# Moving the fetch of the rows' terms and of the first three row tiles from behind the second group's distances to between their stores

## The chip, the cores and the metric

One core of one Trainium2 chip runs the whole program. The metric is device time of one execution in microseconds (us), the median of several runs.

## What is computed

A latent array `x` (32 sequences of 64 rows of 256 numbers) is aligned with a context (32 sequences of 1601 rows of 256), and then passes a recurrence and a mixture of experts. The change lies in the first part, the alignment:

```python
D = sqrt(max(|a|^2 + |b|^2 - 2 a b^T, 0))           # 64 x 1601 distances for each of the 32 sequences
R[i, j] = D[i, j] + min(R[i-1, j], R[i, j-1], R[i-1, j-1])
# the way back: from (63, 1600) to (0, 0), each time to the smallest of the three neighbours
expanded[j] += a[i]   for every (i, j) on the way
x = x + expanded                                     # a = the context rows, summed per latent row
x = x + recurrence(layernorm(x))
x = x + experts(layernorm(x))                        # 8 experts, top 2, and a shared one
```

With the shapes of this case each latent row receives the sum of the context rows that the path matches with it: the "path sums".

## The kernel before, in words

The 32 sequences are worked in two groups of 16, and each group in 32 **units** (u = 0 to 31 for the first group, 32 to 63 for the second). A unit is a pair of sequences and a quarter of the 1601 columns. Per unit:

- SyncE (SP) loads transposed context columns into one of a few `ctxT` tiles; one load (two DMAs, one per sequence) serves two units. In the second group two slots alternate, so a load can only be issued when ScalarE's squares and TensorE's products of the two units that used the slot before are done (`load_next`, which runs at the odd units of SP's loop).
- ScalarE (ACT) squares the columns (`sq`, L1444), TensorE (PE) forms the products (L1734, and L1740 with the squares), and ACT takes the roots (`distance_roots`). PE then subtracts (L1780, L1781) and VectorE (DVE) corrects (L845, `z`) and adds (L861, `dist`).
- SP stores the distances to DRAM (`spaced`, L2226), and loads them back in the layout of the alignment (`table`, L2241).

DVE works through the alignment of the group: 71 steps forward (`align`: L948 the minimum, L959 the scan, L908 `stays`, L914 `code`), then 71 steps of the way back (L977, L978, L984), then `path_features`, which ends in `path_terms` (L1053). Its order is written out by hand: the second group's distances alternate with the first group's `align(0)`, one piece each; the last 14 or so of these units lie beside the first way back. After `path_features(0)` it runs `align(1)`, between whose steps other work is fitted by a table of numbers.

PE's order is fixed as well. Beside `align(1)` it does, for the first group, `path_weigh` (L1812: the path terms times the rows' terms give a mask of which context row belongs to which latent row), and then the path sums (L1834: the mask times the context rows `rows_c`). `BESIDE_SECOND` puts the first two `path_weigh` behind step 4 of `align(1)`, and the first sums behind step 10, that is behind the first half of `code_gap` of the second four steps (L1757, L1758), which needs DVE's `code` tile of L914 at step 10.

The operands of that work are fetched by SP: `first_terms` (416 KB, a copy back from DRAM of what was made at the start) and the ring of `rows_c` tiles, of which n = 0, 1 and 2 have no earlier user in the ring (896, 896, and 640 plus 65 KB). They lie over the first group's table, so they may land only once its coding is done (`coded` at `CODES`). SP issues all its DMAs in program order and waits in place for each semaphore, and nearly all traffic uses this one queue. In the kernel before, SP comes to these four loads after the last unit: it stores the last distances, loads the last table rows, issues `xr` (2 MB), and then

```python
            e.wait_ge(coded, CODES)
            e.wait_ge(terms_kept, 16)
            e.dma_start(first_terms[:, :], kept_terms[:, :]).then_inc(terms_in, 16)
            for n in range(3):
                load_rows(n)
```

Of the kernel before, what the change touches and what calls it, by code (L numbers as in the profile page):

```python
# [33 lines left out]
GUNITS = UNITS // GROUPS  # L34
# [5 lines left out]
CTH = -(-CT // 2)  # L40
ROWS_RING = 5

BEHIND_CODES = 4
LATE_PIECES = 1
ROWS_RING2 = ROWS_RING + BEHIND_CODES + 2
HD = 16
# [8 lines left out]
CODES = -(-STEPS // CB)  # L55
# [127 lines left out]
def run(steps):  # L183
    for _ in steps:
        pass
# [84 lines left out]
def rows_slot(n):  # L270

    return n % ROWS_RING if n < 2 * B // GROUPS else (n - 2 * B // GROUPS) % ROWS_RING2


def rows_before(n):

    return max((m for m in range(n) if rows_slot(m) == rows_slot(n)), default=None)
# [59 lines left out]
def build(nc, x, ctx_nat, ctx_tr, wr_t, wk, wv_t, ww_t, wo_t, gate_t, w1_t, w3_t, w2_t, out):  # L337
    stack = ExitStack()
    with stack:
# [4 lines left out]
        kept_terms = nc.dram_tensor("kept_terms", (P, CT * P), F16).ap()  # L344
# [7 lines left out]
        def place(name, free, dt=F32):  # L352
            size = int(np.prod(free)) * mybir.dt.size(dt)
            at = cursor[0]
            cursor[0] += size + (-size) % 32
            assert cursor[0] <= nc.sbuf_usable_end, (name, cursor[0], nc.sbuf_usable_end)
            return nc.alloc_sbuf_tensor_at(name, [P] + list(free), dt, offset=at)
# [68 lines left out]
        def at(offset):  # L426
            cursor[0] = offset
# [4 lines left out]
        for g in range(GROUPS):  # L432
# [49 lines left out]
        at(table_at[1] + SLOTS * W * 2)  # L482
        rows_c += [place(f"rows_c{i}", [CTH, D]) for i in range(ROWS_RING, ROWS_RING + BEHIND_CODES)]
        assert cursor[0] <= table_at[1] + TABLE
        at(work_at)
        rows_c += [place(f"rows_c{i}", [CTH, D]) for i in range(ROWS_RING + BEHIND_CODES, ROWS_RING2)]
        assert cursor[0] <= align_end
# [5 lines left out]
        first_terms = place("first_terms", [CT * P], F16)  # L493
# [70 lines left out]
        step_done, stayed, gapped, barred, edged, coded, back_done, termed, spread = (  # L564
            sem(n) for n in ("step_done", "stayed", "gapped", "barred", "edged", "coded", "back_done", "termed", "spread"))
        differed = sem("differed")
        numbered, shaped, terms_kept, terms_in = sem("numbered"), sem("shaped"), sem("terms_kept"), sem("terms_in")
# [53 lines left out]
        def stored(e, u):  # L621

            for m in range(u - DISTS + 1, u + 1):
                e.wait_ge(dist_out[m % DISTS], dist_slot_value(m))

        def load_lanes(e, c):

            r0, r1 = CHUNK_ROWS[c], CHUNK_ROWS[c + 1]
            lanes = bass.AP(spaced[0].tensor, r0 * W, [[LANE, P // SETS], [P // SETS * LANE, SETS], [1, (r1 - r0) * W]])
            e.dma_start(table[0][:, 1 + r0:1 + r1, :].rearrange("p r c -> p (r c)"), lanes).then_inc(table_in[c], 16)  # L630
# [1539 lines left out]
        def sync_program(e):  # L2170
# [11 lines left out]
            def load_rows(n):  # L2182
                if n >= 2 * B:
                    return
                pair, half, b = n // 4, n // 2 % 2, n % 2
                i, r0, r1 = rows_slot(n), half * CTH * P, min(N, (half + 1) * CTH * P)
                full = (r1 - r0) // P
                m = rows_before(n)
                if m is not None:
                    e.wait_ge(rows_read, 2 * (m // 4) + m // 2 % 2 + 1)  # L2190
                e.dma_start(rows_c[i][:, 0:full, :], ctx_nat[2 * pair + b][r0:r0 + full * P, :].rearrange(
                    "(t p) d -> p t d", p=P)).then_inc(rows_in[i], 16)
                if r0 + full * P < r1:
                    e.dma_start(rows_c[i][0:r1 - r0 - full * P, full, :],
                                ctx_nat[2 * pair + b][r0 + full * P:r1, :]).then_inc(rows_in[i], 16)
# [23 lines left out]
            def store_distance(u):  # L2219

                pair, q = divmod(u, QUARTERS)
                i = u % DISTS
                e.wait_ge(dist_done, u + 1)
                for b in range(2):
                    at_lane = pair_of(pair)[b] % GB * SEGS * LANE + 2 * q * (LANE + W)
                    e.dma_start(bass.AP(spaced[u // GUNITS].tensor, at_lane, [[W, T], [LANE + W, 2], [1, W]]),  # L2226
                                overlapping(dist[i][b * T:(b + 1) * T, :])).then_inc(dist_out[i], 16)

            def load_table(pair):

                g = pair // GTILES
                first = LOADED_WITH[pair % GTILES]
                sets = range(2 * first // QUADS, (2 * pair % GB + 2) // QUADS)
                e.wait_ge(cleared, g + 1)
                e.wait_ge(padded, PADDED)
                for i in range(DISTS):
                    e.wait_ge(dist_out[i], dist_slot_value(QUARTERS * pair + i))
                for c in range(ROW_CHUNKS):
                    r0, r1 = CHUNK_ROWS[c], CHUNK_ROWS[c + 1]
                    for i in sets:  # L2240
                        e.dma_start(table[g][i:P:SETS, 1 + r0:1 + r1, :].rearrange("p r c -> p (r c)"),  # L2241
                                    spaced[g][32 * i:32 * (i + 1), r0 * W:r1 * W]).then_inc(table_in[c], 16)
                    yield
# [14 lines left out]
            def store_pads():  # L2258

                e.wait_ge(filled, 1)  # L2260
                for g in range(GROUPS):
                    e.dma_start(bass.AP(spaced[g].tensor, T * W, [[SEGS * LANE, GB], [LANE + W, SEGS - 1], [1, PAD]]),
                                far[0:PADS, :]).then_inc(padded, 16)

            def load_next(n):
                for m in following(n):
                    e.wait_ge(ctx_read, 2 * n + 2)
                    e.wait_ge(squared, 2 * n + 2)
                    load_ctxT(m)

            loading = iter(())
            for u in range(UNITS):
                if u % 2 and u != GUNITS + 1:
                    load_next(u // 2)
                if u == QUARTERS:
                    store_pads()
                if u % GUNITS:
                    store_distance(u - 1)
                    pair, g = u // QUARTERS - 1, u // GUNITS
                    if g and u % QUARTERS == 1 and pair % GTILES in LOADED_WITH and pair // GTILES == g:  # L2280
                        run(loading)
                        loading = load_table(pair)
                    for _ in range(2):
                        next(loading, None)
                if u == QUARTERS + 2:
                    e.wait_ge(shaped, SHAPED)
                    e.dma_start(kept_terms[:, :], made_terms[:, :]).then_inc(terms_kept, 16)
                if u == GUNITS - 1:
                    store_distance(u)
                    stored(e, u)  # L2290
                    e.wait_ge(terms_kept, 16)
                    for c in range(1, ROW_CHUNKS):
                        load_lanes(e, c)
                        if c == 4:
                            load_next(GUNITS // 2)
                elif u == UNITS - 1:
                    store_distance(u)
                    run(loading)
                    run(load_table(u // QUARTERS))
# [1 line left out]

            e.wait_ge(product, UNITS)
            e.dma_start(xr[:, :, :], x_tiles).then_inc(x_in, 16)

            e.wait_ge(coded, CODES)
            e.wait_ge(terms_kept, 16)
            e.dma_start(first_terms[:, :], kept_terms[:, :]).then_inc(terms_in, 16)
            for n in range(3):
                load_rows(n)

            e.wait_ge(dist_done, UNITS)
            for i in range(DISTS):
# [71 lines left out]
        scalar_program(nc.scalar)  # L2384
        tensor_program(nc.tensor)
        sync_program(nc.sync)


# [18 lines left out]
```

## Time and profile before

| | us |
|---|---|
| median of 3 runs | 1099.56 |
| the three runs | 1094.05, 1099.56, 1312.1 |
| the profiled execution, its own time | 1102.49 |
| its span, first to last instruction | 1100.3 |
| PE busy in the span | 962.6 (87%) |
| DVE busy | 651.5 (59%) |
| ACT busy | 497.9 (45%) |

The span is 2.2 us shorter than the execution's own time. PE is busy for most of the run, but the first 590 us or so hold two alignments, in which DVE works through long chains of short dependent steps, so the busy shares of the whole run say little about the stretch in which the change lies, 275 to 360 us.

### The profile page before, as it was taken

Reading aid. Unit: us, or ns where it says so; the run is one execution under the profiler, and the core shown is the slowest. Engines: PE = TensorE matmul, PEld = TensorE weight load, DVE = VectorE, ACT = ScalarE, POOL = GpSimd, SP = SyncE. Lnnn points to the kernel's source line nnn. Section 1 sums busy time; section 2 is a strip of 40 time slices with the busy share of each in tenths; the row PEclk is TensorE's granted clock in tenths of the full one; section 3 lists DMA queues with packets and bytes.
Section 4 is the critical chain, followed back from the end, with each engine's and each line's share of the span. In section 5 each row is a group of like instructions: output and inputs, shape, how many; then the busy total and the mean of one; then the engine's idle time right before and its main releaser. Section 6 shows DMA issues by size and latency. Waiting matters only on the chain.

```text
span 1100.3 us, 15331 instructions
## 1 busy us (share of the span) xinstructions
PE 962.6 (87%) x4784; PEld 575.5 (52%) x4784; DVE 651.5 (59%) x2329; ACT 497.9 (45%) x851; POOL 115.8 (11%) x150
## 2 busy tenths in 40 slices
PE   5999788889953879749997998898999999999999
PEld 2334333333311445526764646475767676776776
DVE  7898799998899886898984224365111111111116
ACT  6899577777731555335313652431322222222222
POOL 2000000000000000000000000002334343342110
PEclk9999899999985989859998997888999999999999
DMA  9999895656859997420602963951213121223015
GB/s 353 299 361 337 273 325 150 198 165 189 249 146 328 298 327 236 144 66 1 199 1 68 356 201 108 352 206 52 63 53 91 49 89 60 83 63 113 25 48 201
DMA packets 123822, 190.46 MB, mean 173 GB/s; under 512 B 8800, under 2 KB 92928, under 8 KB 123744
## 3 DMA queue, kind: packets, MB, share of 16 engines
q1 hardware_dynamic: 117712, 170.72, 47.8%
q0 software_dynamic: 5888, 18.36, 5.5%
q8 instruction: 41, 0.67, 0.3%
q10 hardware_dynamic: 144, 0.41, 0.1%
q14 instruction: 37, 0.30, 0.1%
HBM read 165.43 MB, written 24.03 MB: 172 GB/s over the span
## 4 chain that ended last, share of the span: by engine, by line
PE 64%; DVE 20%; ACT 6%; DMA 4%; issue 4%; SPq 2%; POOL 0%; ACTq 0%; DVEq 0%; POOLq 0%
PE bank L1987 14%; PE bank L1834 8%; PE bank L2018 8%; PE bank L1855 5%; PE bank L1740 4%; DVE beyond L978 4%; PE bank L1979 3%; DVE passed L984 3%; PE bank L1998 3%; PE bank L2010 3%; PE bank L1761 3%; ACT sq L1444 2%; PE bank L1762 2%; DMA spaced<-dist 2%; PE bank L1982 2%
## 5 line engine op out<-in xcount | busy, mean ns | idle before, releaser
L1170 DVE TENSOR_TENSOR hid<-bank,act_s 128x352 f32<-128x352 f32 x104 | 54.2, 523 | 216.2 <-PE bank L1987 178.8
L1987 PE MATMUL bank<-w_up,srcT 128*128 x512 | 162.8, 460 | 0.8 <-ACT srcT L1595 0.8
L1603 ACT ACTIVATE act_s<-bank 128x352 f32<-128x352 f32 x104 | 48.0, 463 | 203.2 <-PE bank L1987 115.6
L1987 PEld LDWEIGHTS bank<-w_up,srcT 128*128 128x128 f32 x512 | 96.0, 189 | 48.0 <-issue 4.1
L1740 PE MATMUL bank<-sq,ones 128*64 128x402 f32 (+1 forms) x512 | 101.7, 518 | 18.9 <-ACT sq L1444 18.8
L1834 PE MATMUL bank<-rows_c,on_path 128*64 128x256 f32 (+1 forms) x832 | 103.4, 403 | 5.0 <-DMA rows_c<-ctx_nat_dram 4.5
L1734 PE MATMUL bank<-ctxT,latT 128*64 128x402 f32 (+1 forms) x512 | 101.8, 519 | 4.7 <-DMA ctxT<-ctx_tr_dram 3.9
L1444 ACT ACTIVATE sq<-ctxT 128x1608 f32<-128x1608 f32 x64 | 97.6, 1528 | 11.2 <-DMA ctxT<-ctx_tr_dram 11.1
L2018 PE MATMUL bank<-w_dn,hidT 128*128 (+1 forms) x384 | 93.6, 380 | 0.4 <-DVE y_sb L1184 0.4
L959 DVE TENSOR_TENSOR_SCAN table<-col_min,table 128x201 f32<-128x201 f32 x140 | 88.6, 633 | 1.9
L1611 ACT ACTIVATE hidT<-bank 128x384 f32<-128x384 f32 x104 | 51.0, 490 | 77.0 <-PE bank L1998 76.9
L1834 PEld LDWEIGHTS bank<-rows_c,on_path 128*64 128x64 f32 (+1 forms) x832 | 61.9, 145 | 41.9 <-issue 14.0
L1979 PE MATMUL bank<-ws_up,h2T 128*128 128x352 f32 x256 | 82.7, 471 | 0.0
L1740 PEld LDWEIGHTS bank<-sq,ones 128*64 128x64 f32 x512 | 35.2, 140 | 79.1 <-ACT sq L1444 44.3
L2018 PEld LDWEIGHTS bank<-w_dn,hidT 128*128 128x128 f32 (+1 forms) x384 | 68.2, 191 | 7.3 <-issue 0.6
L1510 ACT ACTIVATE on_path<-bank 128x512 f32<-128x512 f32 x32 | 19.1, 597 | 103.9 <-PE bank L1812 103.9
L1734 PEld LDWEIGHTS bank<-ctxT,latT 128*64 128x64 f32 x512 | 34.6, 139 | 59.3 <-issue 52.3
L634 POOL IOTA tile_io<- 128x36 f32 x1 | 0.2, 162 | 612.0 <-DVE weight L1160 612.0
L1979 PEld LDWEIGHTS bank<-ws_up,h2T 128*128 128x128 f32 x256 | 49.7, 196 | 24.5 <-issue 2.5
L1489 ACT ACTIVATE code<-bank,unpassed 128x402 bf16<-128x402 f32 x72 | 41.4, 588 | 44.8 <-PE bank L1763 40.3
L978 DVE SCALAR_TENSOR_TENSOR beyond<-row,threshold 128x201 f32<-128x201 f16 x142 | 59.8, 421 | 0.0
L1998 PE MATMUL bank<-ident,hid 128*128 128x128 f32 (+1 forms) x312 | 52.3, 277 | 4.9 <-ACT hidT L1611 3.2
(310 smaller groups left out, 1593.3 us busy)
## 6 DMA issues: line engine op xcount, KB each, us to landing
rows_c<-ctx_nat_dram SPq DMA_DIRECT2D x32, 896.0 KB
ctxT<-ctx_tr_dram SPq DMA_DIRECT2D x32, 804.0 KB, 7.9
ctxT<-ctx_tr_dram SPq DMA_DIRECT2D x32, 797.0 KB, 7.9
rows_c<-ctx_nat_dram SPq DMA_DIRECT2D x32, 640.0 KB
spaced<-dist SPq DMA_DIRECT2D x128, 101.0 KB, 5.0
w_up<-w_t_dram SPq DMA_DIRECT2D x16, 704.0 KB, 13.4
table<-spaced SPq DMA_DIRECT2D x7, 808.0 KB, 12.7
table<-spaced SPq DMA_DIRECT2D x28, 202.0 KB, 3.8
```

Of the source, the lines that this page charges most:

```text
L959: e.tensor_tensor_scan(cur[:, 1:W], low, cur[:, 1:W], first, ALU.min, ALU.add).then_inc(step_done, 1)
L978: e.scalar_tensor_tensor(beyond[:, 0:L], row2[:, 0:L], old, row2[:, 0:L], ALU.is_lt, ALU.mult).then_inc(back_done, 1)
L1170: e.tensor_tensor(hid[i][:, :], psum[2 * i + 1][:, 0:HH], act_s[i][:, :], ALU.mult).then_inc(hid_done, 1)
L1444: e.activation(sq[i][:, :, :, 0:nq], ctxT[ctx_slot(n)][:, :, :, q * QC:q * QC + nq], ACT.Square).then_inc(squared, 1)
L1734: last = e.matmul(ps[b * T:(b + 1) * T, 0:nq], latT[:, k, pair * P + b * T:pair * P + (b + 1) * T], ctxT[ctx_slot(n)][:, b, k, half * QC:h ...
L1740: last = e.matmul(ps[b * T:(b + 1) * T, 0:nq], ones[:, 0:T], sq[i][:, b, k, 0:nq], start=False, stop=(k == KC - 1))
L1834: last = e.matmul(psum[pair % 2][b * T:(b + 1) * T, 0:D], on_path[(2 * pair + half) % 3][0:k, t - half * CTH, b * T:(b + 1) * T], rows_c[r ...
L1855: last = e.matmul(psum[bank][:, :], w[:, k, oc * P:(oc + 1) * P], hT[:, k, :], start=(k == 0), stop=(k == KC - 1))
L1979: last = e.matmul(psum[2 * i + m][:, 0:HH], shared_x(t, k), ws_up[:, m, k, columns], start=(k == 0), stop=(k == KC - 1))
L1987: last = e.matmul(psum[2 * i + m][:, 0:HH], srcT[t % 2][:, k, :], w_up[:, bass.ds(ex, 1), m, k, columns], start=(k == 0), stop=(k == KC - 1))
L1998: last = e.transpose(psum[6][0:r, c * P:(c + 1) * P], hid[i][:, c * P:c * P + r], ident[:, :])
L2018: last = e.matmul(psum[7][:, 0:D], hidT[i][0:r, c, :], w_dn[0:r, bass.ds(ex, 1), half * HC3 + c, :], start=first_c, stop=last_c)
```

## The change

SP's loop over the units gets two more branches, and the block behind it is dropped. At u = `ROWS_AHEAD` = 54, after the store of unit 53, SP waits for `coded` and issues `first_terms`; at u = 55, 56 and 57, after the stores of units 54, 55 and 56, it issues the three row loads. No byte more or less is moved.

```diff
+ROWS_AHEAD = GUNITS + 22
...
+                if u == ROWS_AHEAD:
+                    e.wait_ge(coded, CODES)
+                    e.dma_start(first_terms[:, :], kept_terms[:, :]).then_inc(terms_in, 16)
+                elif ROWS_AHEAD < u <= ROWS_AHEAD + 3:
+                    load_rows(u - ROWS_AHEAD - 1)
...
             e.wait_ge(product, UNITS)
             e.dma_start(xr[:, :, :], x_tiles).then_inc(x_in, 16)
-
-            e.wait_ge(coded, CODES)
-            e.wait_ge(terms_kept, 16)
-            e.dma_start(first_terms[:, :], kept_terms[:, :]).then_inc(terms_in, 16)
-            for n in range(3):
-                load_rows(n)
```

The order of PE, DVE, ACT and GpSimd is the same in both kernels. On SP, the stretch of units 53 to 58 stood like this before (`spaced` are the stores of a unit, two DMAs each; `ctxT` the loads for two units, first those of 58 and 59, then those of 60 and 61, then those of 62 and 63; `table` rows of the second table):

```order
L2226 DMA spaced<-dist_147 64x2x202 x2
L2175 DMA ctxT_135<-ctx_tr_dram 128x2x797 x2
L2226 DMA spaced<-dist_148 64x2x202 x2
L2226 DMA spaced<-dist_149 64x2x202 x2
L2175 DMA ctxT_134<-ctx_tr_dram 128x2x804 x2
L2226 DMA spaced<-dist_146 64x2x202 x2
L2241 DMA table_108<-spaced 32x808 x2
L2226 DMA spaced<-dist_147 64x2x202 x2
L2241 DMA table_108<-spaced 32x1616 x2
L2175 DMA ctxT_135<-ctx_tr_dram 128x2x797 x2
```

and stands like this now (lines are numbered one higher here):

```order
L2227 DMA spaced<-dist_147 64x2x202 x2
L2291 DMA first_terms<-kept_terms 128x1664
L2176 DMA ctxT_135<-ctx_tr_dram 128x2x797 x2
L2227 DMA spaced<-dist_148 64x2x202 x2
L2192 DMA rows_c_157<-ctx_nat_dram 128x7x256
L2227 DMA spaced<-dist_149 64x2x202 x2
L2192 DMA rows_c_158<-ctx_nat_dram 128x7x256
L2176 DMA ctxT_134<-ctx_tr_dram 128x2x804 x2
L2227 DMA spaced<-dist_146 64x2x202 x2
L2242 DMA table_108<-spaced 32x808 x2
L2192 DMA rows_c_159<-ctx_nat_dram 128x5x256
L2195 DMA rows_c_159<-ctx_nat_dram 65x256
```

The terms and the first two row tiles have moved ahead of the `ctxT` load of units 60 and 61, and the third row tile ahead of that of units 62 and 63. Behind the last unit, SP's queue read before:

```order
L2303 DMA xr<-x_dram 128x16x256
L2307 DMA first_terms<-kept_terms 128x1664
L2191 DMA rows_c_157<-ctx_nat_dram 128x7x256
L2191 DMA rows_c_158<-ctx_nat_dram 128x7x256
L2191 DMA rows_c_159<-ctx_nat_dram 128x5x256
L2194 DMA rows_c_159<-ctx_nat_dram 65x256
L2315 DMA w_k<-wk_dram 128x2x256
```

and reads now:

```order
L2309 DMA xr<-x_dram 128x16x256
L2315 DMA w_k<-wk_dram 128x2x256
L2315 DMA w_r<-wr_t_dram 128x2x256
L2315 DMA w_v<-wv_t_dram 128x2x256
L2315 DMA w_w<-ww_t_dram 128x2x256
```

The five issues are gone from there, and the weights of the recurrence follow `xr` at once.

## Rows read from the trace of the kernel before

**Rows 1.** Who waited for whom, whole run: us in total, times, longest us.

```profile
PE bank L1812 <- DMA first_terms<-kept_terms: 27.5, 1, 27.5
```

**Rows 2.** Instructions of PE in order of time: start, us, and the idle time before.

```profile
344.54 0.91 PE L1812 MATMUL bank<-path_terms,first_terms 128*128 128x128 f16 x7 [27.45 <-DMA first_terms<-kept_terms]
...
352.04 0.49 PE L1757 MATMUL bank<-code,same 128*128 128x402 bf16 x1 [3.30 <-DVE code L914]
...
352.80 5.53 PE L1834 MATMUL bank<-rows_c,on_path 128*64 128x256 f32 x28
```

**Rows 3.** The chain of work that ended last, 330 to 354 us: start, us, what.

```profile
335.55 1.08 DVE path_terms L1053
...
350.99 0.92 DVE code L914
```

**Rows 4.** The same chain, 240 to 350 us: end of the first coding, two corrections.

```profile
251.58 0.47 DVE code L922
...
302.14 0.42 DVE z L845
...
311.14 0.43 DVE z L845
```

**Rows 5.** DMA issues of SP in order of time: start, us until the last was issued.

```profile
276.70 1.08 SPq L2175 DMA_DIRECT2D ctxT<-ctx_tr_dram  x2
279.82 7.33 SPq L2226 DMA_DIRECT2D spaced<-dist  x4
287.25 1.09 SPq L2175 DMA_DIRECT2D ctxT<-ctx_tr_dram  x2
...
297.63 1.04 SPq L2175 DMA_DIRECT2D ctxT<-ctx_tr_dram  x2
...
332.37 4.26 SPq L2307 DMA_DIRECT2D first_terms<-kept_terms  x1
336.67 6.81 SPq L2191 DMA_DIRECT2D rows_c<-ctx_nat_dram  x3
```

**Rows 6.** Instructions of ACT in order of time, 262 to 318 us.

```profile
295.89 1.54 ACT L1444 ACTIVATE sq<-ctxT 128x1608 f32<-128x1608 f32 x1 [2.17 <-DMA ctxT<-ctx_tr_dram]
...
298.60 0.53 ACT L1459 ACTIVATE root<-root 128x395 f32<-128x395 f32 x1
...
305.84 1.55 ACT L1444 ACTIVATE sq<-ctxT 128x1608 f32<-128x1608 f32 x1 [2.23 <-DMA ctxT<-ctx_tr_dram]
```

**Rows 7.** Stretches: length; PE, PEld, DVE, ACT, POOL busy; PEclk, DMA share, GB/s.

```profile
284.40:287.40 3.00, 3.00 (x18) 1.21 (x13) 2.85 (x16) 2.97 (x4) 0.00 (x0) 1.00 0.12 32
...
295.20:297.00 1.80, 1.80 (x6) 0.68 (x4) 1.65 (x11) 1.11 (x1) 0.00 (x0) 1.00 0.37 91
297.00:299.60 2.60, 2.60 (x17) 1.06 (x16) 2.53 (x13) 2.50 (x5) 0.00 (x0) 1.00 0.89 171
...
358.40:360.40 2.00, 2.00 (x23) 1.39 (x23) 0.53 (x1) 1.50 (x3) 0.00 (x0) 1.00 0.41 114
360.40:369.60 9.20, 7.12 (x50) 3.64 (x48) 7.66 (x24) 4.70 (x10) 0.00 (x0) 0.81 1.08 340
```

**Rows 8.** PE in order of time, 285 to 375 us: the subtraction of unit 59.

```profile
299.86 0.93 PE L1780 MATMUL bank<-z,ident 128*128 128x395 f32 x2
300.63 0.83 PE L1781 MATMUL bank<-root,less 128*128 128x395 f32 x2
```

**Rows 9.** DMA issues by size, whole run: KB each, us to landing.

```profile
rows_c<-ctx_nat_dram SPq DMA_DIRECT2D x32, 896.0 KB
```

**Rows 10.** PE in order of time, 374 to 460 us: a wait for rows.

```profile
376.11 3.24 PE L1834 MATMUL bank<-rows_c,on_path 128*64 128x256 f32 x28 [1.74 <-DMA rows_c<-ctx_nat_dram]
```

**Rows 11.** The distance stores: us to landing, those issued from 290.4, then from 312.0.

```profile
DMA to landing us min/median/max: 4.8/5.1/5.5
...
DMA to landing us min/median/max: 2.3/2.3/2.3
```

**Rows 12.** The ctxT loads of units 60 and 61, issued from 287.3: us to landing.

```profile
DMA to landing us min/median/max: 5.7/6.9/8.0
```

## The prediction

> **What bounds the kernel now.** I first read the list of waits, because the change makes something arrive earlier and so can only pay where somebody waits for it. One wait answers to it: TensorE waits 27.5 us, once, for `first_terms` [rows 1]. The reader should not take this for 27.5 us to be had. TensorE's order of time shows the wait from 317.1 to 344.54 us, then the first `path_weigh`, and then a second wait, of 3.30 us up to 352.04, whose releaser is DVE's `code` tile of L914; only behind that stand the path sums, at 352.80 [rows 2]. So I read the chain of waits next: from 330 to 352 us it lies on DVE, through `path_terms` (335.55 plus 1.08, so 336.6 us) and the first steps of `align(1)` to the `code` tile, which ends at 350.99 + 0.92 = 351.91 us; from there it crosses to TensorE [rows 3]. No transfer stands in it between 335 and 352 us.
>
> The other half of the question is the place to which the fetches go. There I read SP's issues [rows 5], ScalarE's and TensorE's order of time [rows 6, 8] and the load on the DMA engines in stretches of a few microseconds [rows 7]. What the reader should see: ScalarE waits for the `ctxT` load of units 60 and 61 until 295.89 us (2.17 us) and for that of units 62 and 63 until 305.84 us (2.23 us) [rows 6]. These loads are late already, and DVE, whose corrections depend on them, is the bound of this stretch with little room.
>
> **What the removal gives.** `first_terms` would be there before it is needed, so the first `path_weigh` runs when `path_terms` is ready: at about 336.7 instead of 344.54 us, 7.8 us earlier. What is late next is the `code` tile: its 351.91 us is made by DVE alone, in steps that wait for nothing of TensorE or ScalarE [rows 3]. The sums start at 352.8 us as before. Worth: 0.
>
> The four fetches also leave the traffic behind the last unit: 416 KB, twice 896 KB, and 640 plus 65 KB, together 2913 KB or 2.98 MB. At the 340 GB/s that row loads reach [rows 7] that is 8.8 us of the DMA engines. Who is freed by that? The next row loads (n = 5 and on) are issued when a sum has released a slot, after 358.3 us, and the DMA engines run nearly dry just then: share 0.41 from 358.4 to 360.4 us [rows 7]. So the backlog ends before they start, and TensorE's wait of 1.74 us for rows at 376.11 [rows 10], which begins and ends behind it, stays. Worth: 0. SP itself gains 4.26 + 6.81 us of issuing [rows 5] plus the tail of the third tile, and then waits for others anyway.
>
> **What the addition costs.** The price of one fetch in DMA time, at 340 GB/s [rows 7]: `first_terms` 0.43 MB, 1.25 us; a row tile of 896 KB [rows 9], 0.92 MB, 2.7 us; the third, 0.72 MB, 2.1 us.
>
> Does a DMA have to wait for those issued before it? The distance stores say so: the one issued at 290.4, behind a `ctxT` load, takes 4.8 to 5.5 us to land, the one at the end of the stretch, with nothing before it, 2.3 us [rows 11]. The Trainium skill ("DMA: Bandwidth & Descriptors", section "Queues, rings and completion order") says that each DMA engine takes its descriptors in ring order; by that rule the two row tiles delay the load behind them in full, and the trace agrees with its 2.3 against 4.8 us.
>
> Now in SP's order:
> - `first_terms` goes out at about 276.7 us, just ahead of the `ctxT` load of units 58 and 59 [rows 5]. The coding that it waits for ended at 252 us [rows 4], so that wait is none. The load lands 1.25 us later. ScalarE, TensorE and DVE have not been waiting for it; I cost it at nothing as such, and it uses up room in the hole that follows.
> - The hole: from 284.4 to 287.4 us the DMA share is 0.12 [rows 7], which leaves 3.0 x 0.88 = 2.6 us. The terms and row tile 0 (issued behind the stores of unit 54, about 281 us [rows 5]) want 1.25 + 2.7 = 3.95 us. 1.3 us spill over.
> - Row tile 1 is issued at about 287.2 us, just before the `ctxT` load of units 60 and 61 [rows 5]: 2.7 us more. That load lands 1.3 + 2.7 = 4.0 us later, at about 299.9 instead of 295.89 us (its second DMA took 8.0 us to land with nothing ahead of it [rows 12]).
> - Row tile 2 (2.1 us) stands before the `ctxT` load of units 62 and 63 (issued 297.63 [rows 5]). Between the two loads the DMA engines have 1.8 x 0.63 + 2.6 x 0.11 = 1.4 us free [rows 7]. That load lands 4.0 + 2.1 - 1.4 = 4.7 us later, at about 310.5 instead of 305.84 us.
>
> What that does to DVE: from the landing to the end of ScalarE's second root it takes 298.60 + 0.53 - 295.89 = 3.24 us [rows 6], and TensorE's two subtractions another 300.63 + 0.83 - 299.86 = 1.6 us [rows 8]. After the first load that gives 299.9 + 3.24 + 1.6 = 304.7 for a correction that DVE began at 302.14 us [rows 4]: 2.6 us late (its slack was 302.14 - 301.46 = 0.7 us). After the second: 310.5 + 3.24 + 1.6 = 315.4 for one begun at 311.14 us [rows 4]: 4.2 us late, the first 2.6 us among them. These corrections stand between the steps of the first way back in DVE's fixed order, so the way back, `path_terms` and all of `align(1)` are 4.2 us late, and behind them the sums, and from 352 us on the chain has no hole in which it could be made good.
>
> The bounds. Below: with the DMA engines at the 4 to 12% more that short stretches might give, and the hole used in full (3.0 us), the delay of the second load falls to about 3 us, and DVE's to 2.7 us. Above: SP is held in the issue itself. Behind `xr` the terms took 4.26 us and the three row issues 6.81 us [rows 5]; if the issue of row tile 1 holds SP for half of 6.81 us, 3.4 us, the load behind it is issued that much later, and the sum is 7.6 us. I take the middle sum, since far fewer bytes stand in the queue at 281 us than behind the 2 MB of `xr`, and round it to 4 us.
>
> **The sum.** 0 + 0 + 4 = 4 us. On the profiled execution: 1102.49 + 4 = 1106.5 us, span 1104.3. The profiled time stands 2.9 us over the median; on the median it is 1099.56 + 4 = 1103.6, and I say 1103.5 us.
>
> **The rivals.**
> 1. *The hidden fetch* (no effect). The DMA engines have room between 276 and 310 us, and if the DMA engines interleave the transfers kindly, the two `ctxT` loads lose less than DVE's 0.7 us slack. For it: a mean DMA share of about 0.7 over the stretch. Against it: that ScalarE waits for both loads today, and the landing times of the stores [rows 6, 11]. Time: 1099.6 us.
> 2. *The early sums* (faster). If the path sums began when their operands are there, the gain would be the 7.8 us between 336.7 and 344.54: 1091.8 us. A small form: the two early `path_weigh` bring TensorE's clock up sooner. The 28 matmuls at 352.80 took 5.53 us, the 28 at 376.11 took 3.24 us [rows 2, 10], the clock granted being the lower of the two levels (1.2 GHz) in the first case; half of the difference would be worth about 1 us, all of it 2.3 us: 1097.3 us. Against the large form: the 3.30 us wait for DVE [rows 2]. It decides only if that wait is not real. The small form can as well go the other way, since the whole sequence moves against the clock's changes.
> 3. *SP held in its issues* (clearly slower). The place is the issue of row tiles 0 and 1 between the stores of units 54 to 56; the price 3.4 us for each tile that meets a full queue. With one such hold 7.6 us, 1107.2 us; with two 11 us, 1110.6 us. It decides from the point at which an issue takes more than the 0.6 us or so that DMA issues of this stretch take.
>
> That the change does not do what it says, I give no chance of its own: SP meets no unfinished semaphore at u = 54 [rows 4].
>
> **How the numbers follow.** My forecast, 3 to 5 us slower: 0.5. Hidden fetch: 0.2. Faster by early sums or clock: 0.13. Held issues: 0.15. Something else: 0.02. The range: the three cases other than the large gain and the double hold give 1097 to 1107; the runs shown lie 5.5 us apart (1094.05 and 1099.56), so I add some 2.5 us at either end: 1095 to 1110. A measurement of this kernel can tell about 2%, 22 us, from no change. No case reaches that: faster 0.01, within 2% 0.96, slower 0.03.
>
> **What would show it.** In the profile after: the wait of TensorE for `first_terms` gone, the first `path_weigh` right behind `path_terms`; then TensorE waiting for DVE's tiles until about 356 us, and the sums at about 357 instead of 352.8 us. ScalarE's waits for `ctxT` near 296 and 306 us grown by some 4 and 1 us. DVE with new gaps near 303 and 313 us. SP's four row issues between 281 and 294 us at under 1 us each. The waits for rows near 376 us as long as before, only shifted. I am wrong if `path_terms` stands within 1 us of 336 us, or if the sums start before 352 us.

## The result, and the profile after

| | kernel before | changed kernel |
|---|---|---|
| median of 20 runs, us | 1096.74 | 1100.91 |
| ratio to before, 95% interval | | 1.0038 (1.0019 to 1.0056) |
| the profiled execution, us | 1102.49 | 1093.12 |
| its span, us | 1100.3 | 1091.9 |

The changed kernel is slower by 0.38%, 4.2 us between the medians, within the 2% that the forecast called no change. The profiled execution of the changed kernel happens to be the shortest of its 20 runs, and that of before is above all but one of its own; so the two spans must not be compared, only the order and the durations inside them. Points in time of the two profiles can't be compared either: the last `code` instruction of the first coding, where nothing differs yet, starts at 251.58 us before and at 249.12 us after.

The four issues do what the diff says. SP's issues in order of time (start, us until the last was issued), after:

```profile
274.62 0.59 SPq L2291 DMA_DIRECT2D first_terms<-kept_terms  x1
275.32 0.90 SPq L2176 DMA_DIRECT2D ctxT<-ctx_tr_dram  x2
...
279.17 0.62 SPq L2192 DMA_DIRECT2D rows_c<-ctx_nat_dram  x1
...
283.56 0.60 SPq L2192 DMA_DIRECT2D rows_c<-ctx_nat_dram  x1
284.26 1.12 SPq L2176 DMA_DIRECT2D ctxT<-ctx_tr_dram  x2
...
290.28 0.58 SPq L2192 DMA_DIRECT2D rows_c<-ctx_nat_dram  x1
...
294.37 1.81 SPq L2176 DMA_DIRECT2D ctxT<-ctx_tr_dram  x2
```

Each issue holds SP for some 0.6 us (the rest of the third tile, in a DMA of its own, 0.74 us); the 4.26 and 6.81 us that they took behind `xr` [rows 5] are gone. The first issue behind `xr` is now that of the weights `w_k`, and it holds SP for 4.27 us. TensorE in order of time, after:

```profile
333.51 0.93 PE L1813 MATMUL bank<-path_terms,first_terms 128*128 128x128 f16 x7 [18.52 <-DVE path_terms L1054]
...
343.65 0.49 PE L1758 MATMUL bank<-code,same 128*128 128x402 bf16 x1 [7.25 <-DVE code L915]
...
349.85 0.50 PE L1758 MATMUL bank<-code,same 128*128 128x402 bf16 x1 [4.71 <-DVE code L915]
...
350.61 5.23 PE L1835 MATMUL bank<-rows_c,on_path 128*64 128x256 f32 x28
```

The wait of 27.45 us for the terms [rows 2] has become one of 18.52 us for `path_terms`. What TensorE won there it waits away again for DVE's `code` tiles, 7.25 and 4.71 us, where it waited 3.30 us before. From the start of `path_terms` to the first sums it is 350.61 - 333.17 = 17.4 us, and was 352.80 - 335.34 = 17.5 us.

ScalarE in order of time, and then the landing times of the two DMAs of the load of units 60 and 61 (those issued at 284.3), after:

```profile
294.90 1.55 ACT L1445 ACTIVATE sq<-ctxT 128x1608 f32<-128x1608 f32 x1 [3.62 <-DMA ctxT<-ctx_tr_dram]
...
303.74 1.54 ACT L1445 ACTIVATE sq<-ctxT 128x1608 f32<-128x1608 f32 x1 [1.12 <-DMA ctxT<-ctx_tr_dram]
```

```profile
DMA to landing us min/median/max: 8.6/9.3/10.0
```

The load takes 10.0 us to land, against 8.0 us [rows 12]; ScalarE waits 3.62 us for it, against 2.17, and 1.12 us for the next one, against 2.23 [rows 6]. VectorE shows the consequence, a gap at the correction of unit 59 that it didn't have before (before, then after), and the chain of waits now runs through that load:

```profile
302.06 0.56 DVE L845 TENSOR_TENSOR z<-bank,slope 128x395 f32<-128x395 f32 x1
```

```profile
299.90 0.57 DVE L846 TENSOR_TENSOR z<-bank,slope 128x395 f32<-128x395 f32 x1 [1.43 <-PE bank L1782]
```

```profile
284.91 9.97 DMA ctxT<-ctx_tr_dram
```

The hole that the forecast counted on is full (stretches, columns as in [rows 7]; there the DMA shares were 0.12 and 0.37):

```profile
284.40:287.40 3.00, 3.00 (x18) 1.21 (x18) 2.90 (x14) 2.90 (x6) 0.00 (x0) 1.00 1.13 338
295.20:297.00 1.80, 1.79 (x12) 0.59 (x10) 1.72 (x11) 1.77 (x3) 0.00 (x0) 1.00 1.13 379
```

### The profile page after: what moved, and what is told of

Its sections match the earlier page's. It is cut to its first block, busy times and chain, and to the rows that moved or that the text cites. A ratio compares the mean times of both kernels' runs of the same rounds, so it can differ in the third digit from the quotient of the medians.

```text
span 1091.9 us, 15330 instructions
## 1 busy us (share of the span) xinstructions
PE 953.1 (87%) x4784; PEld 569.8 (52%) x4784; DVE 650.7 (60%) x2329; ACT 497.9 (46%) x851; POOL 115.9 (11%) x150
## 4 chain that ended last, share of the span: by engine, by line
PE 67%; DVE 17%; ACT 7%; DMA 4%; issue 4%; SPq 1%; POOL 0%; ACTq 0%; DVEq 0%; POOLq 0%
PE bank L1988 14%; PE bank L1835 8%; PE bank L2019 8%; PE bank L1856 5%; PE bank L1741 5%; PE bank L1980 5%; PE bank L1999 3%; ACT sq L1445 3%; PE bank L1762 3%; PE bank L2011 3%; DVE beyond L979 3%; PE bank L1763 2%; DVE passed L985 2%; PE bank L1735 2%; PE bank L1983 2%
## 5 line engine op out<-in xcount | busy, mean ns | idle before, releaser
L1741 PE MATMUL bank<-sq,ones 128*64 128x402 f32 (+1 forms) x512 | 99.5, 510 | 20.7 <-ACT sq L1445 20.6
L1980 PE MATMUL bank<-ws_up,h2T 128*128 128x352 f32 x256 | 85.7, 484 | 0.0
```

The lines of the kernel that those rows point to most:

```text
L1741: last = e.matmul(ps[b * T:(b + 1) * T, 0:nq], ones[:, 0:T], sq[i][:, b, k, 0:nq], start=False, stop=(k == KC - 1))
L1980: last = e.matmul(psum[2 * i + m][:, 0:HH], shared_x(t, k), ws_up[:, m, k, columns], start=(k == 0), stop=(k == KC - 1))
```

## The experiments

The first comparison (before, changed) is of 20 runs each; the medians of the other kernels are of 12 runs, those of copies_twice and sums of 6. The ratio is to the kernel before on the same chip, with its 95% interval. "Stretch" is, from the profile, the start of VectorE's last `code` instruction of the first coding to the start of `path_terms`: all that the four fetches can delay before their operands are used. The experiments ran on three chips, on which the medians of before, of 29 to 35 runs, were 1096.5 (again, late, copies, sums), 1097.2 (null, copies_twice, moved, moved_late_rows_first) and 1096.9 us (the others).

| kernel | median, us | ratio | stretch, us | landing of the load of units 60, 61 |
|---|---|---|---|---|
| before | 1096.7 | | 83.76 | 8.0 |
| null | 1097.60 | 1.0000 (0.9970 to 1.0030) | 82.82 | 6.9 |
| changed | 1100.91 | 1.0038 (1.0019 to 1.0056) | 84.05 | 10.0 |
| again | 1098.80 | 1.0021 (0.9988 to 1.0054) | 85.26 | 10.3 |
| again_2 | 1098.47 | 1.0022 (1.0004 to 1.0039) | 85.59 | 9.8 |
| late | 1095.90 | 0.9998 (0.9963 to 1.0032) | 84.23 | 7.0 |
| late_2 | 1095.50 | 0.9999 (0.9975 to 1.0023) | 82.84 | 6.9 |
| copies | 1100.32 | 1.0031 (1.0007 to 1.0055) | 86.47 | 11.2 |
| copies_twice | 1111.08 | 1.0108 (1.0058 to 1.0159) | 92.99 | 12.2, issued 2 us later |
| sums | 1108.09 | 1.0115 (1.0074 to 1.0156) | 83.77 | 9.6 |
| moved | 1096.35 | 0.9981 (0.9950 to 1.0012) | 83.72 | 10.0 |
| moved_before | 1099.45 | 1.0025 (1.0001 to 1.0048) | 85.27 | 7.3 |
| moved_late_rows_first | 1094.21 | 0.9963 (0.9929 to 0.9997) | 84.65 | 8.4 |
| best_2 | 1093.74 | 0.9976 (0.9955 to 0.9997) | 84.23 | 8.3 |

**null, again, again_2: how much one profile says.** The kernel before and the changed kernel, unedited.

> The kernel before, unchanged, for a second profile of it and for the size of the noise. Both theories: ratio 1.000 within 0.003. Theory A (delayed context loads): from the end of the first coding to path_terms 83.5 to 85 us, with VectorE's regular step of 4.5 us per unit broken once or not at all. If that stretch scatters here by 2 us, one profile of each kernel can not carry the reading.

> The changed kernel once more, for a second profile beside the first. Theory A (delayed context loads): ratio to the kernel before about 1.004; the context load of units 60 and 61 lands 10 us or more after its first issue, against 8.6 us before, and VectorE has a gap of 1 to 1.5 us near the correction of unit 59. Rival B (TensorE's clock): the slower median comes from where TensorE's low-clock stretches fall, so the ratio is anywhere between 0.998 and 1.006 and the VectorE gap does not tell it.

> The changed kernel a third time, beside the late fetch on the same chip. In four profiles with its fetches in place, the stretch from the end of the first coding to path_terms took 83.7 to 85.3 us, in four without them 82.8 to 84.7 us. Theory A (delayed context loads): ratio 1.003 to 1.004, and the load of units 60 and 61 lands 9.5 us or more after its issue. If the ratio comes out at 1.001 or less, the 0.38% of the first comparison is partly chance and the loss is the 0.5 to 1 us that the profiles show.

Null's ratio is uncertain by 0.3% either way, and its stretch, 82.82 us, is 0.9 us shorter than in the first profile of the same kernel and outside the 83.5 to 85 us that I had expected. The two repeats of the changed kernel are slower by 0.21% and 0.22%, below the 0.4% and the 0.3 to 0.4% expected; so the 0.38% of the first comparison was at the upper end. Again alone does not exclude 1.000. The load lands in 10.3 and 9.8 us, as expected. In again VectorE's gap is 3.05 us, more than the 1 to 1.5 us expected, in again_2 1.22 us.

The stretch can be taken apart. In each profile it is 82.1 us of VectorE's own work, to within 0.2 us, plus what VectorE waits in it, and nearly all of that is at the corrections of units 55, 59 and 61 (idle time of VectorE, us; a dash is under 0.3):

| kernel | unit 55 | unit 59 | unit 61 |
|---|---|---|---|
| before | 1.53 | - | - |
| null | - | - | 0.61 |
| late | - | - | 2.03 |
| late_2 | - | - | 0.38 |
| moved_before | 0.59 | - | 2.40 |
| moved_late_rows_first | 2.43 | - | - |
| best_2 | 1.53 | - | 0.43 |
| changed | - | 1.43 | - |
| again | - | 3.05 | - |
| again_2 | 2.11 | 1.22 | - |
| sums | - | 1.07 | 0.42 |
| moved | - | 1.49 | - |
| copies | - | 4.01 | - |
| copies_twice | - | 10.60 | - |

The wait at unit 59 is there in all five kernels with the fetches ahead of the loads, 1.65 us in the mean, and in none of the seven without. The wait at unit 61 is the other way round, 0.08 against 0.84 us in the mean. The wait at unit 55 hangs on the load of units 56 and 57, which is issued before any of the fetches; it comes and goes in both groups and hides a part of the difference of the stretches. By these waits the fetches cost 1.65 + 0.08 - 0.84 = 0.9 us.

**late: the same fetches behind the last context load.**

```diff
-ROWS_AHEAD = GUNITS + 22
+ROWS_AHEAD = GUNITS + 28
```

> The same fetches four loop steps of units later (first terms at the store of unit 59, row tiles behind those of 60 to 62), so behind the last context load. The operands are still there before path_terms. Theory A: no context load is delayed, so the loss goes and nothing is gained: ratio 1.000, within 0.001 or so. Rival B: the rest of the program moves as in the changed kernel, ratio about 1.004. Rival C (early operands pay after all): below 0.998.

> The fetches behind the last context load once more. Theory A: ratio 0.999 to 1.001 and 2 to 4 us below the changed kernel on the same chip. Rival: as slow as the changed kernel, within 1 us.

Twice 1.000, and 2.9 and 3.0 us below the changed kernel on the same chip. The operands are still early (TensorE's first `path_weigh` waits for `path_terms` alone), no context load has a fetch before it, and no loss is left that these runs can tell from nothing: in late_2 the load of units 60 and 61 lands in 6.9 us, and ScalarE hardly waits for it. Its landing times and ScalarE's order of time:

```profile
DMA to landing us min/median/max: 5.4/6.1/6.9
```

```profile
292.00 1.54 ACT L1445 ACTIVATE sq<-ctxT 128x1608 f32<-128x1608 f32 x1 [0.37 <-DMA ctxT<-ctx_tr_dram]
303.73 1.55 ACT L1445 ACTIVATE sq<-ctxT 128x1608 f32<-128x1608 f32 x1 [3.98 <-DMA ctxT<-ctx_tr_dram]
```

This fits both zeros of the forecast, early terms and relieved traffic, to within their intervals, 3.8 and 2.6 us either way, and says that the place is what costs. Late against changed is clear of noise in only one of the two pairs; VectorE's wait at unit 59, which is gone in both, is the firmer sign. Late_2 shows one thing more: the load after it, of units 62 and 63, makes ScalarE wait 3.98 us here, without any fetch ahead of it.

**copies, copies_twice: the cost alone, and doubled.** The fetches stay where they were before; copies that nobody reads are added.

```diff
+                if GUNITS + 23 <= u <= GUNITS + 25:
+                    j = u - GUNITS - 23
+                    e.dma_start(spare[j, :, :].rearrange("(t p) d -> p t d", p=P),
+                                ctx_nat[j][0:7 * P, :].rearrange("(t p) d -> p t d", p=P)).then_inc(spare_in, 16)
```

(copies_twice: two of them in each of the three places.)

> The kernel before, with its fetches where they were, and three extra DRAM to DRAM copies of 896 KB each behind the stores of units 54 to 56, which nobody reads. Theory A: the cost alone without the removal, 2 to 5 us, ratio 1.002 to 1.005 (a copy between two DRAM places may take longer than a load, so rather the upper end). Rival B: 1.000 or no relation. If the removal from behind the last unit had been worth something, this one would be slower than the changed kernel by that.

> As the kernel with three extra copies, but six copies of 896 KB, two behind each of the stores of units 54 to 56. Theory A: the idle time of the DMA engines is used up by the first three, so the other three delay the two context loads by their full time, at least 2.7 us each and twice that if a copy inside DRAM costs read and write: ratio 1.007 to 1.020, and the loss is seen as gaps of VectorE before path_terms. Rival B (TensorE's clock, not the loads): ratio near that of three copies, 1.003, and no such gaps.

Three copies lengthen the stretch to 86.47 us, some 2.5 us over the mean of the seven kernels with nothing ahead of the loads (83.97 us), and the run by 0.31%. Six lengthen it to 92.99 us, 9.0 us over that mean, and the run by 1.08%. The rise is steeper than in proportion: the first 2.75 MB find room in part, the next find none. With six copies SP is held in its issues too, as rival 3 of the prediction had it: the second two copies take 2.97 us to issue and the two DMAs of the load 3.83 us, where in copies one copy takes 0.61 us and the load 1.15 us. So the load is issued 2 us later, its second DMA 2 us later still, and what the queue and what the hold costs of the 9.0 us isn't separated. Copies was also to tell what the removal is worth: it is 1.5 us above again, and its stretch 1.2 us longer, so it doesn't show that the removal gains anything. Stretches of copies_twice (columns as in [rows 7]), and VectorE's gap:

```profile
290.00:294.00 4.00, 3.62 (x18) 1.30 (x14) 3.81 (x22) 1.96 (x4) 0.00 (x0) 1.00 1.09 296
294.00:298.00 4.00, 0.00 (x0) 0.00 (x0) 3.82 (x19) 0.00 (x0) 0.00 (x0) 0.99 1.07 364
298.00:302.00 4.00, 0.00 (x0) 0.00 (x0) 1.17 (x7) 0.00 (x0) 0.00 (x0) 0.50 1.05 377
```

```profile
309.84 0.57 DVE L847 TENSOR_TENSOR z<-bank,slope 128x395 f32<-128x395 f32 x1 [10.60 <-PE bank L1783]
```

The DMA engines are full at 296 to 377 GB/s, TensorE and ScalarE stand still from 294 us, and VectorE follows. TensorE's granted clock is still 0.99 from 294 to 298 us, where TensorE does nothing, and 0.50, the lower level of 1.2 GHz, from 298 to 302 us. The rival that only the clock's phase makes the difference expected six copies to cost what three do and no gap of VectorE; as the cause of what the copies cost it falls.

**sums, moved, moved_before: can the early operands be used?** `BESIDE_SECOND` gives the pieces of work behind each step; TensorE and ScalarE follow it.

```diff
 BESIDE_SECOND = [int(n) for n in (
-    "000010000021110021110201110400000100320020112202121012022002032010000200"
+    "000030000021110021110201110400000100320020112202121012022002032010000200"   (sums)
+    "000030000001110021110201110400000100320020112202121012022002032010000200"   (moved, moved_before)
```

> The changed kernel, with two pieces of the work beside the second alignment moved from step 10 to step 4: the first pair's path sums and what follows two pieces earlier on TensorE and ScalarE, VectorE's order untouched. If the sums are held only by the place in the order, they start at about 338 us instead of 351, in TensorE's idle time: I expect VectorE's wait of 2.7 us for the first sum to go and 2 to 5 us gained against the changed kernel, ratio to the kernel before 0.998 to 1.001. Rival: the context rows' transfers or the coding matmuls that now come behind the sums take it back, ratio 1.004 or more.

> The changed kernel, with the first pair's two path sums moved from behind step 10 of the second alignment to behind step 4, and all later pieces left where they were. The sums start at about 338 us against 351. The second sum needs row tile 3, which is issued behind xr and the weights and came 4.3 us late in the kernel that moved everything. If the shift of all later pieces was what cost the 1.1%, the ratio to the kernel before falls to 1.003 or less; if the late row tile was, it stays near 1.01.

> The kernel before with its fetches where they were, and only the first pair's sums moved from behind step 10 to behind step 4 of the second alignment. Here the operands are what ends the wait: the terms land at 344.5 us and the rows of the second half some 10 us later, and the coding matmuls of the first steps now stand behind them. I expect the sums to end near 358 us or later, VectorE to wait for ScalarE's coding, and a ratio of 1.002 to 1.010: the early fetch is then what makes the moved sums possible. Rival: ratio 0.998 as with the early fetch, which would say that the early fetch is worth nothing even for them.

Sums was expected to gain and lost 1.15%. Its edit adds two pieces behind step 4 and takes none away at step 10, so the whole table runs two pieces ahead of VectorE's; who waited for whom on VectorE, 440 to 520 us:

```profile
DVE code L923 <- ACT code L1495: 12.0, 5, 7.6
```

VectorE waits 12.0 us there for coding that ScalarE does behind the early pieces; the changed kernel has no such wait in that stretch. Moved takes the two pieces back at step 10, and the loss is gone: 0.9981, with an interval that reaches 1.0012. Here the first sums start behind the first masks, and the second sum waits 3.16 us for row tile 3, which is issued behind `xr` and the weights (TensorE in order of time):

```profile
338.10 5.83 PE L1835 MATMUL bank<-rows_c,on_path 128*64 128x256 f32 x28 [0.18 <-ACT on_path L1515]
...
347.59 5.39 PE L1835 MATMUL bank<-rows_c,on_path 128*64 128x256 f32 x24 [3.16 <-DMA rows_c<-ctx_nat_dram]
```

The same move without the early fetch (moved_before) is slower, 1.0025, as expected. VectorE waits 7.6 us for ScalarE's coding, against 1.5 us in moved, and TensorE waits for rows in both places, after 26.30 us for the terms:

```profile
348.39 5.13 PE L1834 MATMUL bank<-rows_c,on_path 128*64 128x256 f32 x28 [2.49 <-DMA rows_c<-ctx_nat_dram]
...
356.69 2.81 PE L1834 MATMUL bank<-rows_c,on_path 128*64 128x256 f32 x24 [2.66 <-DMA rows_c<-ctx_nat_dram]
```

So the early fetch is worth something, some 0.4% between these two (on two chips, each against its own kernel before), but only to an order that asks for the operands before step 10.

**moved_late_rows_first, best_2: a version that beats both.** Moved, with `ROWS_AHEAD = GUNITS + 28`, and:

```diff
             e.wait_ge(product, UNITS)
+            e.wait_ge(back_done, BACK_INCS)
+            for n in range(3, ROWS_RING):
+                load_rows(n)
             e.dma_start(xr[:, :, :], x_tiles).then_inc(x_in, 16)
...
-            e.wait_ge(back_done, BACK_INCS)
-            for n in range(3, ROWS_RING):
-                load_rows(n)
```

> The best version that I see: the first pair's sums behind step 4, the four fetches behind the last context load, and row tiles 3 and 4 issued before xr and the weights. No context load is delayed, and the sums run in TensorE's idle time before 350 us: VectorE's wait of 2.7 us for the first sum goes. I expect 2 to 4 us less than the kernel before, ratio 0.996 to 0.998. Rival: what is gained there is lost again to waits for row tiles near 375 us or at the next wait between VectorE and ScalarE, ratio 1.000.

> The version with the sums behind step 4, the fetches behind the last context load and row tiles 3 and 4 ahead of xr, a second time: ratio 0.995 to 0.998 if the first comparison (0.9963) holds, 1.000 if that was chance.

Twice below the kernel before, by 0.37% and 0.24%, both intervals below 1. TensorE in order of time, best_2:

```profile
337.37 5.55 PE L1835 MATMUL bank<-rows_c,on_path 128*64 128x256 f32 x28 [0.18 <-ACT on_path L1515]
...
343.35 2.81 PE L1835 MATMUL bank<-rows_c,on_path 128*64 128x256 f32 x24
```

No wait for rows, and both sums done at 346.2 us, where the kernel before had not yet begun the first. VectorE's wait for the first sum, 2.7 us before and 2.4 us after, is not there in either profile of this version. After, from 340 to 380 us:

```profile
DVE xr L1064 <- PE bank L1835: 2.4, 1, 2.4
```

Two things differ from moved, the place of the fetches and that of row tiles 3 and 4; which of them gives how much was not run.

## Why the prediction was right, and where its working was not

**The removal, 0: right.** The first `path_weigh` came forward, DVE's `code` tile ended the next wait, and the sums kept their 17.4 us behind `path_terms`. The wait for rows near 376 us was not shortened: after, TensorE waits 2.46 and 0.73 us at the two places (the first for VectorE), against 1.74 us for rows [rows 10] and 0.97 us before. late, with ratios of 0.9998 and 0.9999, shows the sum of these terms, to within its intervals.

**The mechanism of the loss: right for the first of the two loads, wrong for the second.** The fetches delay the load of units 60 and 61, VectorE gets a gap at the correction of unit 59, in all five profiles, and the price goes with the place (late) and the amount (copies, copies_twice). The load of units 62 and 63 did not carry the delay on. Counted from the start of the last `code` instruction of the first coding, ScalarE squares unit 60 at 45.8 us in the five kernels with the fetches ahead and at 43.1 us in the seven without, 2.7 us later; it squares unit 62 at 54.7 and 54.3 us, 0.3 us later. The issue of that load did not move with the load before it, it stands at 45.1 us in the five and at 45.6 us in the seven, and ScalarE waited for it anyway. So of ScalarE's two waits, forecast to grow by some 4 and 1 us, the first grew from 2.17 to 3.62 us and the second shrank from 2.23 to 1.12 us, and the forecast gap of VectorE near 313 us did not come.

**Its size in the stretch: too large, in two terms.** "That load lands 4.0 us later": it landed in 10.0, 10.3, 9.8, 9.6 and 10.0 us in the five kernels with the fetches ahead of it, against 8.0, 6.9, 7.0, 6.9, 8.4, 8.3 and 7.3 us in the seven without, 9.9 against 7.5, so 2.4 us later. In the two holes the DMA engines moved 338 and 379 GB/s and left no idle time, so the holes took up more than I gave them at 340. "Lands 4.7 us later", of units 62 and 63: it landed in 8.0 us from its issue in the first profile after, against 7.6 before, and over five profiles against seven in 8.7 against 8.1 us. The third row tile was all but free. And I added to the gap what was partly there already: in late_2 and null VectorE loses 0.4 and 0.6 us at unit 61, in late 2.0 us, with nothing ahead of that load. The sum "4.2 us" for VectorE measures, over five profiles against seven, 84.48 - 83.97 = 0.5 us in the stretch, with a scatter of some 0.8 us in each group, so the stretch alone would not tell the groups apart; by VectorE's waits at units 59 and 61 it is 0.9 us.

**The total, 4 us: near the first measurement by luck.** The medians say 4.2, 2.3 and 1.6 us, the ratios 1.0038, 1.0021 and 1.0022, about 3 us in all; the profiles place 0.9 us of it in the stretch, where the forecast had all 4.

A part of the rest goes with TensorE's clock, whose mean over each run is on record. In the 93 runs of the kernel before that ran beside the experiments, a mean granted clock that is 0.01 lower goes with a run that is 8.6 us longer, and the runs scatter by 1.6 us about that line. The changed kernel, over 43 of its 44 runs (without one of 1109.99 us), is 2.2 us (95% interval 0.9 to 3.5) above them in the mean; its clock is lower by 0.0014, which by that line is 1.2 us, and at equal clock 1.0 us (0.3 to 1.7) is left. By the same line late is at -0.2 us (-1.0 to 0.6), copies at 3.1 and copies_twice at 8.6 us, near the 2.5 and 9.0 us of their stretches.

So the delayed load costs the changed kernel about 1 us, and about as much again comes with a lower clock, which the small form of rival 2 had said could go either way. Whether the change lowers the clock or the runs happened to have it isn't shown: the interval of the 0.0014 is 0.0003 to 0.0025, and behind `path_terms` the profiles show no loss of the changed kernel, but a scatter of several us among profiles of one and the same kernel (from the first `path_terms` to those of the second group it is 253.7 and 251.1 us in the two of before).

**The signs named in advance.** The forecast called itself wrong if `path_terms` stood within 1 us of 336 us or the sums started before 352 us. By these words it was: after, the sums start at 350.61 us, and `path_terms` starts at 336.45 and 335.60 us in again and again_2. But the signs were bound to the times of one profile; in null, the kernel before itself, the sums start at 350.03 us. Counted from the last `code` instruction of the first coding, the sums start at 101.5, 102.7 and 103.0 us in the three profiles of the changed kernel, and at 101.2 and 100.3 us in the two of the kernel before: 1.7 us later in the mean, not the 4.2 us forecast.

**The rivals.** The hidden fetch is nearer than I made it: the stretch hides most of the transfers, though VectorE's wait and the first ratio do not go back to nothing. The mean DMA share over the stretch, which spoke for it and which I gave as about 0.7, is 0.81 from 276 to 310 us. The early sums could not happen in this order, as the 3.30 us wait said; in moved they did. Held issues did not occur in the changed kernel, 0.6 us each; in copies_twice they did. The range, 1095 to 1110, was wider than what the known terms made necessary.

## What to carry to other kernels

Before an operand is fetched earlier, look at what the reader waits for next: here VectorE ended the next wait, and an early operand was worth nothing until the order asked for it. Then look at what stands behind the new issue in the same queue: put it behind the last transfer that somebody waits for, not merely into a stretch where the DMA engines are 80% busy. A delayed transfer need not delay the next one behind it: look whether its issue moves too, and whether its reader waits already. A move in a table that several engines follow must leave the later entries where they were; two pieces ahead throughout cost 1.15%, while the same two pieces moved alone gained some 3 us against the changed kernel.

## What the runs showed that I had not expected

Extra traffic is far from linear in what it costs: three copies of 0.92 MB added 2.5 us to the stretch, six added 9.0 us, in part because SP was then held in its issues.

The first 28 matmuls of the sums, in the same place behind the same wait, took 5.53 us before, 4.50 us in null, 5.23 us after, 4.38 us in again and 4.46 us in late_2. The granted clock goes with it: TensorE starts them at 0.50 (1.2 GHz) after a stretch almost without work (busy 3.0 of 15 us before, 1.8 of 13 us in late_2), and comes to 2.4 GHz earlier or later within them. Stretches from 354 us, before (columns as in [rows 7]):

```profile
354.00:356.00 2.00, 2.00 (x12) 1.11 (x10) 1.96 (x7) 0.00 (x0) 0.00 (x0) 0.50 1.06 330
356.00:358.00 2.00, 2.00 (x16) 1.08 (x12) 1.96 (x6) 0.00 (x0) 0.00 (x0) 0.63 1.09 365
```

and from 350 us, late_2:

```profile
350.00:352.00 2.00, 2.00 (x10) 0.93 (x10) 1.88 (x9) 0.00 (x0) 0.00 (x0) 0.50 0.03 8
352.00:354.00 2.00, 2.00 (x18) 1.18 (x16) 1.96 (x6) 0.00 (x0) 0.00 (x0) 0.75 0.00 0
```

That is 1 us for one of many such starts, between executions of one and the same kernel.
